# Gathers that add in a four-layer graph network: own rows laid in the ring first, every address good, no bounds

## The reference

```python
# L0: attention over each target's edges (uses h[src], h[dst], edge features), relu
# L1: h @ fc.T + b, scaled by out_deg**-0.5, summed over h[src] per dst, * in_deg**-0.5, + h
# L2, L3: two graph convolutions each; an edge list with a loop for every node
def gcn_conv(x, W, b, src, dst, norm, n):
    h = x @ W
    return segment_sum(h[src] * norm[:, None], dst, n) + b
```

## Time and profile before

| | us |
|---|---|
| median of 3 runs | 3210.51 |
| the runs | 3210.51, 3216.2, 3179.88 |
| span of the profiled execution, first to last instruction | 2548.9 |
| busy in it: POOL, DVE, PE, ACT | 1856.4, 1878.0, 1809.8, 1299.9 |

### The profile page before, as it was taken

One profiled execution on the slowest core, in us unless ns is written; L12 is line 12 of the kernel. 1 busy time (PEld: TensorE's weight loads), 2 busy tenths in 40 slices (PEclk: granted clock), 3 DMA queues, 4 the chain that ended last, 5 costly groups with the idle time before them and its releaser, 6 DMA issues.

```text
span 2548.9 us, 26059 instructions
## 1 busy us (share of the span) xinstructions
PE 1809.8 (71%) x6414; PEld 875.1 (34%) x6414; DVE 1878.0 (74%) x3056; ACT 1299.9 (51%) x2694; POOL 1856.4 (73%) x1775
## 2 busy tenths in 40 slices
PE   3788877774996488878888887768888888860000
PEld 1433333322453243333444343433444344430000
DVE  7999987646888378987999788887999799960000
ACT  2767666532886264545666555545666566620000
POOL 5777777766777777756777577756777677777776
PEclk9999998886998699979999889889999899975555
DMA  2344433224776254443344356563434354440000
GB/s 65 102 125 127 118 109 84 68 72 130 232 241 220 82 167 134 134 129 105 118 125 126 106 163 194 175 190 111 123 120 126 114 145 130 133 133 23 22 22 20
DMA packets 240170, 309.75 MB, mean 122 GB/s; under 512 B 86875, under 2 KB 102389, under 8 KB 239896
## 3 DMA queue, kind: packets, MB, share of 16 engines
q1 hardware_dynamic: 183576, 281.76, 34.5%
q0 software_dynamic: 56448, 26.34, 5.8%
HBM read 188.24 MB, written 144.91 MB: 131 GB/s over the span
## 4 chain that ended last, share of the span: by engine, by line
POOL 20%; DVE 19%; PE 17%; issue 12%; ACT 6%; DMA 1%; DVEq 0%; SPq 0%; ACTq 0%; POOLq 0%
POOL mn_ring L515 12%; POOL out_dram L1883 8%; PE bank L1185 5%; DVE mn_total L1567 4%; DVE node_h L1391 4%; PE bank L1189 3%; PE bank L1194 3%; PE bank L1928 2%; PE bank L1179 2%; PE bank L1199 2%; DVE node_h L1436 1%; DVE mn_scaled L1583 1%; ACT node_square L1312 1%; ACT node_std L1296 1%; DVE node_x L1415 1%
## 5 line engine op out<-in xcount | busy, mean ns | idle before, releaser
L515 POOL DMA_INDIRECT mn_ring<-slot_rows,addr_i x980 | 1036.8, 1058 | 398.0 <-issue 293.7
L1185 PE MATMUL bank<-node_x,center 128*128 128x512 f32 x492 | 257.5, 638 | 73.0 <-DVE node_h L1391 68.9
L515 POOL DMA_INDIRECT found<-node_table,look_i x196 | 212.1, 1082 | 86.4 <-issue 63.8
L1194 PE MATMUL bank<-node_h,wconv 128*128 128x512 f32 x492 | 266.4, 625 | 0.3 <-DVE mn_sums L1701 0.3
L1189 PE MATMUL bank<-node_square,mean 128*128 128x512 f32 x492 | 259.7, 610 | 2.7 <-ACT node_std L1291 2.0
L515 POOL DMA_INDIRECT xin<-in_x_dram,src_i x196 | 205.5, 1048 | 71.7 <-issue 59.4
L1312 ACT ACTIVATE node_square<-bank 128x512 f32<-128x512 f32 x246 | 145.7, 592 | 216.1 <-PE bank L1185 215.9
L515 POOL DMA_INDIRECT xin<-in_x_dram,dst_i x196 | 206.8, 1055 | 63.5 <-issue 59.5
L1306 ACT ACTIVATE node_act<-bank,bias 128x512 f32<-128x512 f32 x246 | 168.3, 684 | 160.0 <-PE bank L1194 159.7
L1883 POOL DMA_INDIRECT out_dram<-keep,scat_i x196 | 193.0, 985 | 62.4 <-issue 62.4
L1199 PE MATMUL bank<-node_act,wconv 128*128 128x512 f32 x442 | 230.2, 603 | 2.5 <-ACT node_act L1306 2.5
(11 more groups left out here) (334 smaller groups left out, 3821.8 us busy)
## 6 DMA issues: line engine op xcount, KB each, us to landing
mn_ring<-local SPq DMA_DIRECT2D x120, 256.0 KB, 4.4
out_dram<-node_rows SPq DMA_DIRECT2D x98, 256.0 KB
mn_rin<-res SPq DMA_DIRECT2D x96, 256.0 KB, 3.7
local<-node_rows SPq DMA_DIRECT2D x96, 256.0 KB
slot_rows<-keep SPq DMA_DIRECT2D x96, 256.0 KB, 2.0
mn_fcol<-f_rows SPq DMA_DIRECT2D x192, 128.0 KB
res<-mn_x SPq DMA_DIRECT2D x72, 256.0 KB, 2.7
node_x_in<-in_x_dram SPq DMA_DIRECT2D x64, 256.0 KB, 2.9
```

The costliest lines, as they stand in the source:

```text
L515: return eng.indirect_dma_start(out=dest, out_offset=None, in_=table, in_offset=bass.IndirectOffsetOnAxis(ap=index, axis=0), bounds_check= ...
L1185: pe.matmul(bank[i][:, :], C["center"][:, :], src, start=True, stop=True).then_inc(s["centered"][i], 1)
L1194: pe.matmul(bank[5 if i == 2 else 1][:, :], C["wconv"][:, 2 * i - 4, :], nd.h[i][:, u % 2, :], start=True, stop=True) \
```

## The change

The arrays `slot_rows` and `local` of a stage become the two halves of one DRAM array of 50176 rows (`slots`). A source that is nobody's target gets the address of its own local row, in the second half (`own`, made by a seventh iota on POOL), so every address is good. The gathers and the lookups lose their bound. In B the gather writes all 128 rows and nothing is filled before it. In C to F SP fills the ring's slot from `keep` (SBUF to SBUF) instead of from DRAM, POOL's indirect DMA adds the gathered row to it (`add_tile`), DVE's `gather_sum` is gone, and PE waits for the gather itself. The number of indirect DMAs is the same. The scatters of the result keep their bound.

```diff
-            local=[dram(f"local{i}", (P, COLS)) for i in range(5)],
-            rows=[dram(f"slot_rows{i}", (P, COLS)) for i in range(5)],
+            slots=[dram(f"slot_rows{i}", (2 * P, COLS)) for i in range(5)],
+        D.update(rows=[a[0:P, :] for a in D["slots"]], local=[a[P:2 * P, :] for a in D["slots"]])
...
+                g.iota(own_i[:, :], pattern=[[1, TILES]], base=EPAD + 1, channel_multiplier=TILES).then_inc(s["pool"], 1)
...
-def gather_tile(eng, dest, table, bound, index):
+def gather_tile(eng, dest, table, index):
     return eng.indirect_dma_start(out=dest, out_offset=None, in_=table,
-                                  in_offset=bass.IndirectOffsetOnAxis(ap=index, axis=0),
-                                  bounds_check=bound, oob_is_err=False)
+                                  in_offset=bass.IndirectOffsetOnAxis(ap=index, axis=0))
+def add_tile(eng, dest, table, index):
+    return eng.indirect_dma_start(out=dest, out_offset=None, in_=table,
+                                  in_offset=bass.IndirectOffsetOnAxis(ap=index, axis=0), compute_op=ALU.add)
...
-                    if st == "B":
-                        v.tensor_tensor(rows3(ring[:, k, :], g), rows3(ring[:, k, :], g), scale(C["osc"], g), ALU.mult) \
-                            .then_inc(s["gs"], 1)
-                    else:
-                        v.tensor_tensor(here, here, of_group(keep, g), ALU.add).then_inc(s["gs"], 1)
+                    v.tensor_tensor(rows3(ring[:, k, :], g), rows3(ring[:, k, :], g), scale(C["osc"], g), ALU.mult) \
+                        .then_inc(s["gs"], 1)
...
-                    link(v.tensor_scalar(none[:, 0, :], val[:, 0, :], 0.0, NOWHERE, ALU.is_equal, ALU.mult))
+                    link(v.scalar_tensor_tensor(none[:, 0, :], val[:, 0, :], 0.0, C["own"][:, :], ALU.is_equal, ALU.mult))
...
-                    sp.dma_start(ring[:, k, 0:w_of(g)], of_group(D["local"][layer], g)).then_inc(s["filled"][k], 16)
+                    sp.wait_ge(s["turned"], i - R - n + 1)
+                    sp.wait_ge(s["row"], i - 2 * n + 1)
+                    sp.dma_start(ring[:, i % R, 0:w_of(g)], of_group(keep, g)).then_inc(s["filled"][i % R], 16)
...
-                    if i + R - 1 < len(order):
+                    if 2 * n <= i + R - 1 < len(order):
                         fill(*order[i + R - 1])
...
-                        gather_tile(gp, ring[:, k, j * F:j * F + F], flat(D["rows"][STAGES.index(st) - 1]), bound,
-                                    C["addr"][:, t:t + 1]).then_inc(s["fetched"][k], 16)
+                        here, slots = ring[:, k, j * F:j * F + F], flat(D["slots"][STAGES.index(st) - 1])
+                        if st == "B":
+                            gather_tile(gp, here, slots, C["addr"][:, t:t + 1]).then_inc(s["fetched"][k], 16)
+                        else:
+                            add_tile(gp, here, slots, C["addr"][:, t:t + 1]).then_inc(s["fetched"][k], 16)
...
-                    pe.wait_ge(s["gs"], i + 1)
+                    if i < 2 * n:
+                        pe.wait_ge(s["gs"], i + 1)
+                    else:
+                        pe.wait_ge(s["fetched"][i % R], gathers(i))
```

More of the change, by code:

```diff
@@ L41 @@
 FAR = 1e30
-NOWHERE = float(1 << 20)
 BEYOND = 32768.0
@@ L275, in _ @@
                 link(v.tensor_copy(pnf[:, :], pn[:, :]))
+                link(v.tensor_copy(C["own"][:, :], own_i[:, :]))
                 v.wait_ge(s["named"], 6 * 16)
@@ L526, in fetch_node_rows @@
     index, sem = (C["dst"], H["landed"]["xd_in"][k]) if target else (C["src"], H["landed"]["xs_in"][k])
-    gather_tile(eng, H["xin"][:, k, target * w + j * F:target * w + j * F + F], A["x"], bound, index[:, t:t + 1]) \
+    gather_tile(eng, H["xin"][:, k, target * w + j * F:target * w + j * F + F], A["x"], index[:, t:t + 1]) \
         .then_inc(sem, 16)
@@ L1516, in evicted, with filled_before @@
                 eng.wait_ge(s["x"], x_at(st, g) + 1)
-        def turn(i, first):
-            return (i - first) // R + 1
+        def filled_before(i):
+            return sum(1 for j in range(2 * n, i + 1) if j % R == i % R)
         def gathers(i):
@@ L1709, in _ @@
                 for i, (st, g) in enumerate(order):
-                    if g == 0:
+                    if g == 0 and st in "AB":
                         gather_sum(st, g)
@@ L1714, in _ @@
                         finish(st, g - 1)
-                    if g < n - 1:
+                    if g < n - 1 and st in "AB":
                         gather_sum(st, g + 1)
@@ L1744, in fill @@
                     i = at(st, g)
-                    k = i % R
-                    if st == "A":
-                        return
-                    if i - R >= n:
-                        sp.wait_ge(s["turned"], i - R - n + 1)
-                    else:
-                        sp.wait_ge(s["total"], i - R + 1)
-                    layer = STAGES.index(st) - 1
-                    if layer and g == 0:
-                        kind = LOCAL_ROWS.index(layer)
-                        sp.wait_ge(nd.s["stored"][kind], 16 * LOCALS)
-                    sp.dma_start(ring[:, k, 0:w_of(g)], of_group(D["local"][layer], g)).then_inc(s["filled"][k], 16)
+                    sp.wait_ge(s["turned"], i - R - n + 1)
+                    sp.wait_ge(s["row"], i - 2 * n + 1)
+                    sp.dma_start(ring[:, i % R, 0:w_of(g)], of_group(keep, g)).then_inc(s["filled"][i % R], 16)
                 def fill_kv(st, g):
```

31 lines of the change are left out of this document (17 added, 14 removed).

## The result

The changed kernel takes 3284.81 us (median of 4 runs, 3281.09 to 3287.36) where the kernel before takes 3209.43 (4 runs): a ratio of 1.0267, 95% interval 1.0203 to 1.033. Two repeats on other chips gave 1.0423 (1.0379 to 1.0467) and 1.0323 (1.0272 to 1.0374). It is slower, as forecast, by 75 us to 129 us and not by 220.

What follows compares the result with a forecast made beforehand. The prediction took POOL to bound the stages, with DVE nearly level. Adding cost 235 us and boundaries, fills and DVE gave back 15: +220 us, a time of 3430 us, with 8 in 10 between 3060 and 3850 us.

Steps and rivals of the forecast that it cites:

- The basis: Whole kernel: effects summed on the trace's span of 2548.9 us, then laid on the median of 3210.5 us.
- All of it on the path, since POOL has no slack in C to F: Stages C to F: the add's whole 235 us on 784 gathers lengthens the kernel.
- The add's term: POOL's gathers in C to F: adding costs 0.30 us more each, 235 us on 784 gathers.
- a third access costs a third: POOL's adding gather: a third access costs a third of about 0.93 us of row work, 0.31 us.
- The prediction's aside that doubled reads: POOL's adding gather: with reads alone doubled, the add's 0.30 us would be about half of a gather.
- the add would be nearly free: Reading of a skill page for C to F: the add costs POOL nothing, giving 3190 us; chance 0.15.
- The bounds: 1568 gathers and lookups lose their bound: taken as nothing, up to 0.1 us of gain.
- The rival of cheap bounds and a free add: Gathers and lookups: dropped bounds save 0.1 us each, add nearly free, 3090 us, end near 3060; chance 0.30.
- Boundaries, fills and DVE: Stage boundaries before D and E, fills in F, DVE relieved of its sum: together 15 us gained.
- The DMA rival: C to F: DMA engines become the bound, 3850 us at 2.2 us a gather; no chance of its own.
- Who waits for the gather is now PE: Group heads in C to F: PE waits for the gather, costing nothing while POOL sets the pace.

Runs made afterwards that it cites:

- e1: The kernel before, unchanged, profiled once more on a chip with pauses: 3147.77 us.
- e13: e2 with a useless POOL clear of 128x288 after every gather of C to F, on the chip without pauses: 2659.0 us, ratio 1.0464.
- e6: The kernel before with a useless POOL memset of 128x448 after each of the 784 gathers of C to F: 3114.62 us, ratio 0.9923.
- e5: The changed kernel once more, on another chip: 3268.21 us, ratio 1.0423 to the kernel before.
- e12: The changed kernel with fewer rows per gather: B copies 64, C adds 64, D adds 32, E copies 32, F adds 128; no total time given.
- e15: e2 with POOL at most two groups ahead of the transposes in C to F instead of four, on the chip without pauses: 2537.5 us, ratio 0.9978.
- e3: The kernel before without bounds on the gathers of x and the lookups: 3152.47 us, ratio 1.0051.
- e2: The changed kernel with copying gathers in C to F, DVE summing, no fills, good addresses and no bounds on gathers: 3145.32 us, ratio 1.0043.
- e4: The changed kernel with a never exceeded bound on the 784 adding gathers: 3275.95 us, ratio 1.0477 to the kernel before.
- e7: The changed kernel with DVE's 96 sums of C to F put back on a scratch tile: 3279.26 us, ratio 1.0455 to the kernel before.
- e10: e2 with a useless POOL clear of 128x672 after each gather in half of the groups of C to F: 3061.96 us, ratio 0.9572.
- e18: e15 run again on a chip with pauses: 3093.48 us, ratio 0.9678.

## Why the prediction was wrong in size

**The basis.** "What it gives is laid on the median, 3210.5, since no edit touches the 661.6 us around the span." In no later run is there such time around the span (1.8 us in after, 10.8 in e1). The 661.6 us were time inside the stages and the front on the kind of chip that gave the times: e1's span is 3137.0 us for the same kernel. The numbers themselves should have warned me: a fifth of the time lay in no stage. This step failed first, and the next one with it.

**"All of it on the path, since POOL has no slack in C to F."** It held for the kind of chip of the earlier trace rows: e13's pace is 0.19 us above the 1.36 of before, 150 us for 784 gathers, its boundaries before D, E and F are 17 us shorter, and C to F take 125 us longer than in the first trace. It didn't hold for the chips that were timed. There POOL waited 349.0 us for the ring, 273.8 of them in C to F (e1), where the first trace had 7.5 in C to F, and a pace of 1.69 us cost nothing (e6). POOL's work on the 784 gathers grew by 422 us from e1 to e5, the kernel by 133 us of span: the 273.8 us of waits for the ring are gone in e5, and the boundaries before D, E and F are 45 us shorter. This is where the expected loss went.

**The add's term** was mis-sized: forecast 0.30 us more for each gather, "a third access costs a third". Measured: 1.575 us against 1.034 (e1) is 0.54, against the unbounded copy's 0.99 it is 0.58. The reason failed too. "About 0.93 us of the 1.06 is work on the 128 rows" was argued from a short POOL instruction of another kind; e12 shows 0.9 ns for a copied row ((0.99 - 0.905)/96) and 2.1 ns for an added one ((1.583 - 1.385)/96), the rest fixed. The prediction's aside that doubled reads would make the price about half of a gather was nearer in size, but it too counted rows. The Trainium skill's sentence on the anatomy of a DMA ("DMA: Bandwidth & Descriptors"), that many descriptors can be emitted before their cost shows, agrees with these rows as far as rows go. The prediction drew from it that the add would be nearly free, and that doesn't follow: the premium is there at 32 rows.

Two errors thus partly cancelled, and that the direction came out right is in part luck: on the timed chips it hung on an add that was nearly twice as dear as I had taken it. At the 1.36 us that I forecast for a gather the pace is 1.66 us, and e6 at 1.69 us was no slower than before. With the right add (784 x 0.54 = 423 us) and the old "no slack" the forecast would have been 423 - 15 us above before, further off than mine. For a chip without pauses I estimate 2543 us + (1508 - 1134), about 2920 us, 15% slower: C to F of after last 1508 us (1510.5 to 3018.8) by POOL's pace alone, against e15's 1134. The change itself wasn't run there.

**The bounds** were taken at nothing: right in time (e3, e2), though not in POOL's own work, where they are 0.04 to 0.05 us of each copy. On an added gather they are nothing (e4). The rival of cheap bounds and a free add falls on its second half.

**Boundaries, fills and DVE**, "1.5 + 5 + 7, I take 15 us": the mechanism of a DVE that is level with POOL is right. POOL's waits at the boundaries before D, E and F are 9.4, 16.9 and 10.0 us after, against 16.2, 23.5 and 14.5, 18 us less in sum. (e1 has 23.4, 28.9 and 28.4 there.) But the boundary before C is 47.5 us instead of 30.6: with B's fills gone POOL ends that stage earlier and waits longer, as e2, which has the same B and adds nowhere, shows with 48.1. e7 shows that none of it reached the time by way of DVE. DVE's busy time is 47.3 us below that of the earlier trace rows and 53.8 below e1's 1884.5, not 67; what the rest of its work took more isn't explained.

**The DMA rival** fell: q0 takes 13.3% of the engines. **"Who waits for the gather is now PE"** was right, with 405.6 us.

## What to carry to other kernels

Compare the span of a trace with the measured time before anything is summed. Here 11 us between them meant nothing and 662 us meant that the trace was not of an execution like the timed ones, so that "no slack" read from it was worth nothing for them. Price slack by putting known useless work on the engine: a run or two tell how much is free and whether the next us counts. And when a variant is faster than expected, imitate its timing without its idea (e10) before the idea gets the credit; a producer that runs far ahead through a deep ring can cost more than it covers, as e18 showed for the chips with pauses.

## What the runs showed of the hardware

- The same kernel took 2543 us on one chip and 3136 to 3209 on the others, every run of a chip within 1.2% of its median. The traces have the same work and the same DMA traffic, and differ by pauses of PE, ACT and DVE, alone or together, while POOL's gathers go on, most of all in the front (738 us in e1 against 508). The traces with pauses also hold fewer events of semaphores (21111 against 56550). What causes the pauses wasn't found, nor whether they belong to the chip, to the sitting or to the recording. In C to F the common standstills over 1 us sum to 114 us with POOL up to four groups ahead (e2), 52 with two (e18) and 29 with clears in half of the groups (e10).
- A gather of 128 rows of 256 bytes keeps POOL for 0.97 to 1.03 us without a bound, 1.03 to 1.06 with one and 1.57 to 1.58 when it adds (means of a run). Nearly all of it is fixed: 0.9 ns for a copied row, 2.1 ns for an added one (e12).
- An added row is a packet of its own (144 packets for a gather, against 32).
